# Summing the direct rows once per block, and one more whole product, in a recommendation kernel on one core

## The reference

```python
for idx, (W, b) in enumerate(params):          # W: (39, fields of xk, 128)
    z = relu(einsum('bhd,bkd,hks->bsd', x0, xk, W) + b[None, :, None])
    if idx != last:
        xk = z[:, :64, :]; direct.append(z[:, 64:, :])
    else:
        direct.append(z)
logit = sum(concatenate(direct, axis=1), axis=-1)      # over the 16 numbers d
```

## Time and profile before

| | us |
|---|---|
| median of 3 runs | 1373.23 |
| lowest, highest | 1372.33, 1373.45 |
| the profiled execution | 1374.53 |
| its span, first to last instruction | 1372.7 |
| busy: TensorE, VectorE, GpSimd, ScalarE | 1249.4, 1166.7, 907.7, 655.3 |
| mean granted TensorE clock | 0.994 of full speed |

### The profile page before, as it was taken

The page is one execution under the profiler, slowest core; times in us unless marked ns, Lnnn a source line. Parts: engine busy times, 40 slices in busy tenths (PEclk is TensorE's granted clock), DMA queues, the critical chain, the costliest instruction groups (busy, mean ns, idle before and its releaser), DMA issues.

```text
span 1372.7 us, 15527 instructions
## 1 busy us (share of the span) xinstructions
PE 1249.4 (91%) x4142; PEld 770.8 (56%) x4142; DVE 1166.7 (85%) x1057; ACT 655.3 (48%) x758; POOL 907.7 (66%) x581
## 2 busy tenths in 40 slices
PE   0189999997999999999999999999999999999989
PEld 0045565565665656665665566665655666665643
DVE  1259999997999999999999999999999999999850
ACT  1135554544545454455545454455545454454532
POOL 6648877766777777676777777676777744555520
PEclk9999999998999999999999999999999999999999
DMA  7199777778877777788877777788877777678500
GB/s 178 16 235 229 169 157 188 176 194 167 201 156 161 187 182 194 176 199 206 199 161 165 189 173 194 179 195 206 199 170 154 193 177 191 176 196 193 124 0 0
DMA packets 133861, 233.49 MB, mean 170 GB/s; under 512 B 15891, under 2 KB 23044, under 8 KB 133730
## 3 DMA queue, kind: packets, MB, share of 16 engines
q1 hardware_dynamic: 80333, 146.77, 45.9%
q10 hardware_dynamic: 43522, 83.90, 23.3%
q0 software_dynamic: 9984, 2.58, 2.6%
HBM read 229.33 MB, written 6.23 MB: 172 GB/s over the span
## 4 chain that ended last, share of the span: by engine, by line
PE 41%; POOL 20%; DVE 19%; issue 15%; ACT 3%; DMA 1%; DVEq 1%; ACTq 0%; POOLq 0%
PE z_even L742 18%; PE z_odd L742 14%; POOL gathered L418 13%; DVE whole L634 9%; POOL rest L430 7%; DVE rest L641 4%; DVE whole_psum L634 4%; ACT head L519 2%; PE z_even L749 2%; PE z_odd L749 2%; PE whole_psum L822 2%; DVE part L669 2%; PE x_odd L769 1%; PE x_odd L822 1%; PE x_even L822 1%
## 5 line engine op out<-in xcount | busy, mean ns | idle before, releaser
L430 POOL TENSOR_TENSOR rest<-whole,head 128x1024 fp32r<-128x1024 f32 x256 | 609.3, 2394 | 310.5 <-ACT head L519 298.6
L634 DVE TENSOR_TENSOR whole<-x_banks,x_rep 128x1024 f32<-128x1024 f32 x448 | 535.2, 1216 | 57.7 <-ACT x_banks L494 57.0
L418 POOL DMA_INDIRECT gathered<-in_tbl,idx x312 | 296.5, 950 | 102.8 <-issue 100.1
L519 ACT CAST head<-whole_psum 128x1024 fp32r<-128x1024 f32 x192 | 194.8, 1014 | 347.9 <-DVE whole_psum L634 295.6
L519 ACT CAST head<-whole 128x1024 fp32r<-128x1024 f32 x256 | 269.0, 1051 | 47.7 <-DVE whole L634 20.1
L641 DVE TENSOR_TENSOR rest<-whole_psum,head 128x1024 fp32r<-128x1024 f32 x192 | 234.6, 1222 | 22.1 <-ACT head L519 21.9
L634 DVE TENSOR_TENSOR whole_psum<-x_banks,x_rep 128x1024 f32<-128x1024 f32 x192 | 235.6, 1227 | 10.3 <-DMA x_rep<-x_rows 7.8
L742 PE MATMUL z_odd<-head,w_rest 128*128 128x512 f32 x460 | 205.2, 446 | 25.1 <-POOL rest L430 19.1
L742 PE MATMUL z_even<-head,w_rest 128*128 128x512 f32 x436 | 194.1, 445 | 24.8 <-issue 10.8
L742 PE MATMUL z_odd<-whole,w_whole 128*128 128x512 f32 x400 | 188.5, 601 | 5.5 <-DVE whole L634 5.5
L742 PE MATMUL z_odd<-rest,w_head 128*128 128x512 f32 x460 | 180.2, 392 | 0.0
(11 more groups left out here) (76 smaller groups left out, 890.3 us busy)
## 6 DMA issues: line engine op xcount, KB each, us to landing
x_rep<-x_rows SPq DMA_DIRECT2D x160, 512.0 KB, 10.2
x_rep<-x_rows ACTq DMA_DIRECT2D x160, 512.0 KB, 10.5
x_shift<-x_rows SPq DMA_DIRECT2D x93, 546.0 KB
gathered<-in_tbl,idx POOLq DMA_INDIRECT x312
x_rows<-xt SPq DMA_DIRECT2D x32, 78.0 KB
x_rows<-xt SPq DMA_DIRECT2D x32, 40.0 KB
x_rep<-in_W_top SPq DMA_DIRECT2D x2, 512.0 KB, 11.8
w_k<-in_L_rec_w SPq DMA_DIRECT2D x1, 760.5 KB
```

The costliest lines, as they stand in the source:

```text
L418: nc.gpsimd.indirect_dma_start(gathered[:, f, :], None, tables[f], bass.IndirectOffsetOnAxis(ap=idx[:, f:f + 1], axis=0)).then_inc(s_gathe ...
L430: nc.gpsimd.tensor_tensor(rest[:, split_slot(product)], whole_slot(product), head[:, split_slot(product)].bitcast(F32), ALU.subtract).then ...
L519: nc.scalar.copy(head[:, split_slot(product)], src).then_inc(s_head, 1)
L634: nc.vector.tensor_tensor(out[0:rows, 0:width, :], xk[0:rows, :].unsqueeze(1).to_broadcast([rows, width, N]), x0, ALU.mult).then_inc(s_pro ...
```

## The change

- Layer 2's product 8 is a U instead of a V (KINDS). Six split products a tile become five in layer 2, and the ring's count of U and P products in a block goes from 72 to 76, which 6 does not divide: `ring_place` begins again at slot 0 with each period of 76, and `before_in_place` finds the product that had the slot before.
- TOGETHER is 4. direct01 and direct2 hold a whole block as [b, 16 values of d], written by `relu_by_sample` with a stride of 16 numbers, and read by one reduce of 2048 numbers a partition. `part`, the add and their semaphores are gone; xt and ctx_t share one buffer.
- On VectorE, add_layers01 stands behind product 7 of layer 2 in a block's last tile, add_layer2 behind layer 0's products, ahead of the wait for x2, in a block's first tile.
- On ScalarE: out_layer2 behind six heads of layer 1 instead of three; xt and emb behind three heads, as before, but no longer behind out_layer2; the relus to x1 behind two heads of layer 2 instead of one; layer 0's direct relu behind all five heads of layer 2 instead of right behind them. The load of group 3 follows head P7.
- On TensorE: the transposes stand behind product 0 of layer 1. PE_ORDER is the order as it was.
- On GpSimd: the gathers are 10, 10, 11 and 8 in a block's four tiles of gathering; one behind the second rest of layer 1 (not in the tile with the refill), up to eight behind the fifth, up to two behind each rest of layer 2, and what is left at its end.

```diff
-KINDS = {1: "UVPPUPVPVP", 0: "UUUU", 2: "UUVUPUVPVP"}
+KINDS = {1: "UVPPUPVPVP", 0: "UUUU", 2: "UUVUPUVPUP"}
 ORDER = (1, 0, 2)
+SPLITS = {layer: len(kinds) - kinds.count("U") for layer, kinds in KINDS.items()}
+PE_ORDER = {1: (0, 1, 2, 3, 4, 5, 6, 7, 8, 9), 2: (0, 1, 2, 3, 4, 5, 6, 7, 8, 9)}
...
-GATHERS_BETWEEN = 11
-HEADS_IN_1 = 3
-HEADS_IN_2 = 1
-TRANSPOSES_AFTER = 2
-ADD_2_AFTER = 4
-ADD_01_AFTER = 1
+GATHERS_AFTER = {1: (0, 1, 0, 0, 8), 2: (2, 2, 2)}
+GATHERS_OF_TILE = (10, 10, 11, 8)
+D2_AFTER = 6
+XT_AFTER = 3
+X1_AFTER = 2
+TRANSPOSES_AFTER = 1
+ADD_01_AFTER = 7
...
-TOGETHER = 2
+TOGETHER = TPB
+D0_AFTER = 5
...
-        xt = sb("xt", [FIELDS, 2, N])
+        xt_and_ctx = sb("xt_and_ctx", [HALF + CTX, 2, N])
+        xt = xt_and_ctx[0:FIELDS]
+        ctx_t = xt_and_ctx[HALF:HALF + CTX].rearrange("p a n -> p (a n)")
...
-        direct01 = sb("direct01", [P, TOGETHER, N])
-        direct2 = sb("direct2", [P, TOGETHER, N])
-        part = sb("part", [P, P])
...
+        in_period = TPB * sum(kind in "UP" for kinds in KINDS.values() for kind in kinds)
+        def ring_place(product):
+            return number(*product, "UP") % in_period % WHOLE_SLOTS
...
+        def before_in_place(t, layer, j):
+            now = run_order.index((t.first, layer, j))
+            found = [x for x in run_order[:now] if place_of.get(x) == place_of[t.first, layer, j]]
+            if not found:
+                return None
+            step, layer, j = found[-1]
+            return Tile(step, t.turn), layer, j
         def whole_slot(product):
-            return whole[:, number(*product, "UP") % WHOLE_SLOTS]
+            return whole[:, ring_place(product)]
...
-                for j in split:
+                for n, j in enumerate(split):
                     product = t, layer, j
                     if j == split[-1] and refill is not None:
                         refill()
+                        refill = None
                     pool.wait_ge(s_head, before(t, layer, j, "PV") + 1)
                     nc.gpsimd.tensor_tensor(rest[:, split_slot(product)], whole_slot(product),
                                             head[:, split_slot(product)].bitcast(F32),
                                             ALU.subtract).then_inc(s_rest_p, 1)
-                    if layer == 2 and fields:
-                        gather(fields.pop(0))
-                for f in fields:
-                    gather(f)
+                    for _ in range(GATHERS_AFTER[layer][n] if refill is None else 0):
+                        if fields:
+                            gather(fields.pop(0))
+                while layer == 2 and fields:
+                    gather(fields.pop(0))
...
-                    fields = list(range(k * per_tile, min((k + 1) * per_tile, FIELDS)))
+                    first = sum(GATHERS_OF_TILE[:k])
+                    fields = list(range(first, first + GATHERS_OF_TILE[k]))
...
-                rests(t, 1, fields[:GATHERS_BETWEEN], refill)
-                rests(t, 2, fields[GATHERS_BETWEEN:])
+                rests(t, 1, fields, refill)
+                rests(t, 2, fields)
...
+            def relu_by_sample(direct, t, z_rows, b):
+                d = t.first % TPB * DPT
+                return relu(direct[:, :, d:d + DPT].rearrange("p b d -> p d b"),
+                            z_rows.rearrange("p (d b) -> p d b", d=DPT), b)
...
-                relu(direct2[:, t.first % TOGETHER, :], z_of(t, 2)[:], bias[:, 2:3]).then_inc(s_d2, 1)
+                relu_by_sample(direct2, t, z_of(t, 2)[:], bias[:, 2:3]).then_inc(s_d2, 1)
...
+            def transposed(t):
+                nxt = t.plus(AHEAD)
+                if nxt.first % TPB == 0:
+                    act.wait_ge(s_gather, nxt.blocks(16 * FIELDS, 16 * FIELDS))
+                    wait(act, s_x0, nxt.count(1))
+                    nc.scalar.copy(emb[:], gathered[:].rearrange("p f d -> p (f d)").unsqueeze(1)
+                                   .to_broadcast([P, SPC, FIELDS * DIM])).then_inc(s_emb, 1)
+                act.wait_ge(s_x0, nxt.count(1, 1))
+                wait(act, s_stored, nxt.count(32, -32))
+                nc.scalar.copy(xt[:, nxt.first % 2, :],
+                               x0_bank[nxt.first % 2][0:FIELDS, :]).then_inc(s_xt, 1)
+            def out_layer1(t):
+                zz = z_of(t, 1)
+                act.wait_ge(s_used, before(t, 1, PAIRS))
+                relu(x2_bank[0:HALF, :], zz[0:HALF, :], bias[0:HALF, 1:2]).then_inc(s_x2, 1)
+                relu(x2_bank[HALF:P, :], zz[0:HALF, :], bias[0:HALF, 1:2]).then_inc(s_x2, 1)
+                if t.first % TOGETHER == 0:
+                    wait(act, s_sum01, t.visits(TOGETHER))
+                relu_by_sample(direct01[HALF:P], t, zz[HALF:P, :], bias[HALF:P, 1:2]).then_inc(s_d01, 1)
+            def next_x1(t):
+                zz = z_of(t, 0)
+                act.wait_ge(s_used, before(t, 0, PAIRS0))
+                relu(x1_bank[0:HALF, :], zz[0:HALF, :], bias[0:HALF, 0:1]).then_inc(s_x1, 1)
+                relu(x1_bank[HALF:P, :], zz[0:HALF, :], bias[0:HALF, 0:1]).then_inc(s_x1, 1)
+            def next_direct(t):
+                nxt = t.plus(1)
+                if nxt.first % TOGETHER == 0:
+                    wait(act, s_sum01, nxt.visits(TOGETHER))
+                relu_by_sample(direct01[0:HALF], nxt, z_of(t, 0)[HALF:P, :], bias[HALF:P, 0:1]).then_inc(s_d01, 1)
...
             def body(t):
-                if has_layers12(t):
-                    heads(t, 1, upto=HEADS_IN_1, loads={1: 0, 2: 1} if has_layer0(t) else {})
-                    if t.turn is not None or t.first > 0:
-                        out_layer2(t.plus(-1))
...
-                if has_layers12(t):
-                    heads(t, 1, start=HEADS_IN_1)
-                    zz = z_of(t, 1)
-                    act.wait_ge(s_used, before(t, 1, PAIRS))
...
-                    if t.first % TOGETHER == 0:
-                        wait(act, s_sum01, t.visits(TOGETHER))
-                    relu(direct01[HALF:P, t.first % TOGETHER, :], zz[HALF:P, :],
-                         bias[HALF:P, 1:2]).then_inc(s_d01, 1)
-                    heads(t, 2, upto=HEADS_IN_2)
-                if has_layer0(t):
...
-                    if nxt.first % TOGETHER == 0:
-                        wait(act, s_sum01, nxt.visits(TOGETHER))
-                    relu(direct01[0:HALF, nxt.first % TOGETHER, :], zz[HALF:P, :],
-                         bias[HALF:P, 0:1]).then_inc(s_d01, 1)
-                if has_layers12(t):
-                    heads(t, 2, start=HEADS_IN_2, loads={6: 2, 8: 3, 9: 4} if has_layer0(t) else {})
...
+                    return
+                for n in range(SPLITS[1] + 1):
+                    if n == D2_AFTER and (t.turn is not None or t.first > 0):
+                        out_layer2(t.plus(-1))
+                    if n == XT_AFTER and has_transposes(t):
+                        transposed(t)
+                    heads(t, 1, start=n, upto=n + 1, loads={1: [0], 2: [1]} if has_layer0(t) else {})
+                out_layer1(t)
+                for n in range(SPLITS[2] + 1):
+                    if n == X1_AFTER and has_layer0(t):
+                        next_x1(t)
+                    if n == D0_AFTER and has_layer0(t):
+                        next_direct(t)
+                    heads(t, 2, start=n, upto=n + 1, loads={6: [2], 7: [3], 9: [4]} if has_layer0(t) else {})
...
-                    last = earlier(t, layer, j, "UP", WHOLE_SLOTS)
+                    last = before_in_place(t, layer, j)
...
-                grouped = direct[:].rearrange("p t (d b) -> p b (t d)", d=DPT)
-                if t.first % TPB < TOGETHER:
-                    nc.vector.tensor_reduce(cols, grouped, AX_X, ALU.add).then_inc(done, 1)
-                else:
-                    nc.vector.tensor_reduce(part[:], grouped, AX_X, ALU.add).then_inc(partial, 1)
-                    dve.wait_ge(done, t.visits(TOGETHER))
-                    dve.wait_ge(partial, t.blocks(1, 1))
-                    nc.vector.tensor_tensor(cols, cols, part[:], ALU.add).then_inc(done, 1)
+                nc.vector.tensor_reduce(cols, direct[:], AX_X, ALU.add).then_inc(done, 1)
...
-                    ends = t.first % TOGETHER == 0 and (t.turn is not None or t.first > 0)
-                    layer12(t, 1, x1_bank, {ADD_2_AFTER: lambda: add_layer2(t.plus(-1))} if ends else {})
+                    layer12(t, 1, x1_bank, {})
...
                 if has_layers12(t):
+                    if t.first % TOGETHER == 0 and (t.turn is not None or t.first > 0):
+                        add_layer2(t.plus(-1))
                     dve.wait_ge(s_x2, t.count(2, 2))
                     ends = t.first % TOGETHER == TOGETHER - 1
                     layer12(t, 2, x2_bank, {ADD_01_AFTER: lambda: add_layers01(t)} if ends else {})
...
-                    for j in range(TRANSPOSES_AFTER):
+                    for j in PE_ORDER[1][:TRANSPOSES_AFTER]:
...
```

(21 more changed lines are left out.)

40 lines of the change are left out of this document (14 added, 26 removed).

## The result

The changed kernel takes **1331.64 us** (median of 4 runs, 1328.45 to 1333.16) against 1373.34 of the kernel before beside it: ratio 0.9678, 95% interval 0.9652 to 0.9703. Forecast were 1330 and a range of 1318 to 1354. The profiled execution took 1333.16, its span 1331.3. In the later comparison (five rounds, another set of runs) the same kernel took 1328.93, ratio 0.9682 (0.9656 to 0.9708).

What follows compares the result with a forecast made beforehand. No engine bounds alone: the chain divides over TensorE, GpSimd and VectorE, with 8.6 us of stops in a 154.19 us block. Block 148.8 plus once-only terms gave 43 less than 1374.5, then 1.3 less: 1330 us, range 1318 to 1354.

Steps and rivals of the forecast that it cites:

- Four causes, 8.6 a block: TensorE's stops: sum in mid layer 1, late emb copy, reduce ahead of V2's rest, gathers ahead of P4's rest.
- (a): Layer 2's product 8 becomes U: TensorE gains 0.34 a tile, +1.4 a block; VectorE loses 1.1 a tile.
- (b): VectorE's remaining work: 4.3 ahead in tiles without sums, where it was 1.60; layer 1's stops go, -4.0 a block.
- (c): Sum of layers 0 and 1 as one reduce, 2.4 long (3.9 kept); V6's rest late, +0.9 a block (or +2.4).
- (g): Things free by themselves, among them the ring of whole slots and group 3's load; the last tile's sum costs +1.
- (d): Direct relus' strided writes on ScalarE: 0.68 each may stay or double; covered, so nothing, or 0.7 a block without cover.
- (e): Layer 2's sum in a block's first tile, both sums in one VectorE round: +0.1 a block, +1.5 with slow reduce.
- (f): GpSimd's shorter gather lump brings P4 sooner: -1.7 a block; long gaps -3 once, tiles 0 and 1 -2.
- (h): Small hand-over gaps of 0.1 to 0.3 at products that just arrive: 0.2 a tile, +0.8 a block.
- slow reduces: Rival: the sum's reduce on VectorE stays at the strided rate of 3.9, block 151.7, 1352 us; chance 0.17.
- x_rep loads: Rival: loads for VectorE land at up to 17.2 us and become the limit, 1404 us; chance 0.06.

Runs made afterwards that it cites:

- a_lump: The changed kernel with the gathers as before: 10, 10, 10 and 9 a tile, all behind layer 1's last rest; 1343.63 us, ratio 0.9762.
- b_gathers: The kernel before with only the gathers as in the changed one (10, 10, 11 and 8 a tile); 1362.17 us, ratio 0.9866.
- b_sum: The kernel before with only the sums changed: once a block, arrays by sample, layer 2's sum behind layer 0's products; 1353.27 us, ratio 0.9814.
- b_u8: The kernel before with layer 2's product 8 a U, the ring's places for it and group 3's load behind head P7; 1366.32 us, ratio 0.9918.
- a_order: The changed kernel with ScalarE's order as before and the sum of layers 0 and 1 behind product 1 of layer 2; 1349.11 us, ratio 0.9766.
- a_sum_last: The changed kernel with the sum of layers 0 and 1 behind product 9 of layer 2 instead of product 7; 1331.37 us, ratio 0.9664.
- a_strided: The changed kernel with direct01 and direct2 stored so that the relus write in order and the reduce reads in strides; 1343.61 us, ratio 0.9748.
- a_early: The changed kernel with 26 instead of 13 gathers of block 1 ahead of tile 0, 7 and 6 in tiles 0 and 1; 1325.24 us, ratio 0.9646.
- a_again: The changed kernel itself once more, unchanged, in the last set of runs; 1328.93 us, ratio 0.9682 against the kernel before.
- a_halves: The changed kernel with the sum of layers 0 and 1 in two halves by partitions, in two successive tiles; 1326.07 us, ratio 0.9651.

## Why the prediction was right, step by step

- **Four causes, 8.6 a block.** All four stops are gone. a_lump and b_gathers show that P4's was the gathers' doing (1.4 a block in both, 1.7 forecast), b_sum that layer 1's was the sum in mid layer and that V2's goes in the tile without a sum; emb's goes with the lead alone (b_u8), but comes back with the longer relus in the old order (a_order).
- **(a) The U.** +0.34 forecast for layer 2, +0.39 measured between V8 and U8 (15.12, 15.51).
- **(b) The lead.** Forecast 4.3 in tiles without sums; VectorE waits 2.84 for x2. The rest of the lead goes into waits for heads and x_rep within layer 1, such as 1.11 for a head before 629.92 (so 3.95 in all). Layer 1 at 15.2 throughout: 15.10 to 15.11.
- **(c) The reduce.** R = 2.4 forecast, 2.28 measured, and 3.75 in strides, near the other end of 3.9. The stop: 0.9 forecast, 16.60 - 15.51 = 1.09 measured. Laid beside tile 13, TensorE is 0.88 late behind V6, as forecast, and loses 0.21 more at P9. So the cover at V6 is 2.28 - 0.88 = 1.4, near the 1.5. The ring, which (g) called free after a look at U5, is not free at U8: where no sum stands ahead of it, it waits 0.84 for its slot (a_sum_last).
- **(d) The relus.** Between the two ends, 1.15 for 0.68, and hidden as forecast: tiles without sums take 36.62 with either (a_strided). The new places on ScalarE are part of that (a_order). Here the Trainium skill ("SBUF — State Buffer", the note on SBUF cachelines) agrees on both sides: numbers read in order are cheaper for VectorE by 1.47 a reduce, and numbers written 64 bytes apart dearer for ScalarE by 0.47 a relu.
- **(e) Both sums in one round.** +0.1 forecast, 0 measured: VectorE is not 1.1 late in tile 16 but still waits 0.65 for x2 (before 715.84). With a reduce of 3.75 it does not wait, and V2 is not late either; the 1.5 there was too much.
- **(f) The gathers.** P4's rest waits for its head now, as forecast. The two other terms failed. Tiles 0 and 1 gained 2.3, of which 1.0 is tile 1's share of the settled gain, so 1.3 for the 2 forecast. The long gaps were to give 3 more than the settled gain; tiles 5 and 6 together gained 2.4 where tiles 9 and 10 gained 3.3, so 0.8 less, and tiles 17 and 18, with the second gap, 3.3, so nothing more.
- **(h) failed:** the 0.8 of small gaps a block isn't there; tiles without sums repeat at 36.62. This is most of the difference between 148.8 and 147.6 a block, which makes some 9 us in 7.5 blocks that I gave away.
- **Not foreseen,** and on the other side of the balance: in tile 2 layer 1 took 19.17, 4.1 above the settled 15.10, where it took 16.92 before. TensorE stands 2.13 for emb, before its row at 172.12, and stood 1.26 before. The last gather of block 1, for whose landing emb waits, is issued at 163.22, 4.9 before the tile's start, and was at 161.81, 5.1 before it; what changed is that TensorE asks for emb one product earlier. Behind the stop its granted clock is half of full speed from 173.3 to 176.7, which it wasn't in the kernel before, and this costs 1.6 of the 4.1; the forecast has no term for the clock. a_early takes both away. And the first 90 us differ by 3 between executions of one and the same kernel: tile 0 began at 90.57 in the first trace of the changed kernel and at 87.09 in the second, at 87.03 before. Over all fourteen traces it began between 83.8 and 90.6.

So 1330 against 1331.64 is in large part luck. Against the terms of the sum the profiled execution gained 9.0 more in the blocks and 1.7 more behind tile 31's start; it gained 4.0 less in tile 2, 3.8 less at the long gaps, 3.5 less ahead of tile 0 and 0.7 less in tiles 0 and 1. These are 10.7 one way and 12.0 the other, and but for 0.1 they turn the 42.8 of the sum into the 41.4 of the spans. The mechanism is another matter: the stages of the settled blocks came out within 0.2 us each, and the causes of the four stops hold in the runs that undid or isolated them.

The rivals: slow reduces were worth 12 us by the medians (13.6 between the starts of tiles 1 and 31), not the 22 given to them (a_strided), since V2's cover held. The x_rep loads did not become a bound: ScalarE's land in 9.3, 11.6 and at most 16.1 us (least, median, most), a microsecond more at the median than before, and VectorE's wait for them stayed at about 8 us in all.

## What to carry to other kernels

Where engines take turns at being late, measure each stage's undisturbed length in the trace itself (a block without gathers, a tile without a sum), take the difference as the sum of the stops, and name each stop's cause from the row that ended it. Then ask for every moved step what stands behind it on its own queue and how much cover the next consumer has: moving the sum by two products only moved its stop from V6 to the next layer's P3, and made it longer. A swap that costs the bounding engine a little (the U, 0.39 a tile) can pay if it gives the others a lead. And where the sum of the terms hits the time, lay it beside the tiles one by one: here errors of some 10 us in both directions met.

## What the runs showed of the hardware

**GpSimd's long gap** comes at the same gather in every trace: the 114th of the 312, always in tile 5 (its fifth or sixth gather there, issued between 301 and 313 us), with 9.3 to 11.1 us in thirteen of the fourteen traces and 4.85 in the other. In the four traces of kernels with all ten gathers in one lump (the kernel before, a_lump, b_u8, b_sum) the 227th, 113 later, is 3.1 to 3.3 late as well (773.00 in the kernel before). In the ten others the 227th comes 11 to 14 us after the 226th in any case, so that such a wait would not show. What GpSimd waits for there no row shows. Where it is about 10 long it costs TensorE 8 to 11 us once: in the changed kernel 7.0 as a stop before 318.0, and most of the rest because the granted clock is half of full speed from 313.2 to 323.4. Where it was 4.85 (b_gathers), the clock stayed full and tile 5 lost less than 1 us. It wasn't tried to take the gap away.

**TensorE's clock** fell to half of full speed behind stops of 1.7 us (a_again, tile 2) and 2.1 us (the changed kernel, tile 2; a_strided, three of seven blocks), with matmuls of 512 columns 0.43 apart instead of 0.23. Not every such stop brings it about: it did not come behind the same stop of 2.11 in four blocks of a_strided, nor behind 2.37 in tile 2 of a_halves. What decides that these runs don't show. A stop of that length can thus cost 1.4 to 1.6 us more than its own.
